# A four-stream counting sort and a reordered tail in a graph-network kernel

## The reference

```
L0:  x += segment_sum(h[src] * e, dst) @ W.T + b
L1:  seg_sum, seg_max, cnt of edge_attr (32 wide) by src;
     x += relu([seg_sum, seg_max, seg_sum/max(cnt,1), u] @ W1 + b1) @ W2 + b2
L2:  hw[r] = h @ weight_r[r];  M = segment_sum(hw[etype, src] / deg[dst], dst)
     x += relu(0.2*h + 0.8*M)
L3:  e = leaky_relu(h@attn_l [src] + h@attn_r [dst]); a = segment softmax of e by dst
     x += elu(segment_sum(h[src] * a, dst))
```

## Time and profile before

| | us |
|---|---|
| median of 3 runs | 22321.71 |
| lowest and highest | 22300.97, 22337.59 |
| the profiled execution, its own time | 22388.18 |
| its span in the trace | 22386.5 |

### The profile page before, as it was taken

One profiled execution on the slowest core, in us unless ns is written; L12 is line 12 of the kernel. 1 busy time (PEld: TensorE's weight loads), 2 busy tenths in 40 slices (PEclk: granted clock), 3 DMA queues, 4 the chain that ended last, 5 costly groups with the idle time before them and its releaser, 6 DMA issues. The chain is left out here.

```text
span 22386.5 us, 124954 instructions
## 1 busy us (share of the span) xinstructions
PE 4204.8 (19%) x27624; PEld 3254.6 (15%) x27624; DVE 7606.3 (34%) x21407; ACT 4300.2 (19%) x11114; POOL 13594.0 (61%) x13464
## 2 busy tenths in 40 slices
PE   1113444444444444211111400000000000000000
PEld 1112333333333333100000300000000000000000
DVE  6663333333333333566655211111111322222222
ACT  0001322222222222222222211111111010110110
POOL 5664444444444444566666377777777677777775
PEclk7555555555555555555555655555555555555555
DMA  2110000000000000133333211111111222222221
GB/s 66 43 43 23 15 17 15 15 15 15 17 15 15 15 15 15 64 97 98 96 99 94 63 48 48 48 44 48 48 44 47 37 45 49 49 46 49 49 45 43
DMA packets 577819, 984.93 MB, mean 44 GB/s; under 512 B 308591, under 2 KB 360528, under 8 KB 541776
## 3 DMA queue, kind: packets, MB, share of 16 engines
q0 software_dynamic: 430432, 388.76, 9.8%
q10 hardware_dynamic: 34560, 436.30, 4.8%
q1 hardware_dynamic: 112368, 155.91, 2.4%
HBM read 458.57 MB, written 521.52 MB: 44 GB/s over the span
## 5 line engine op out<-in xcount | busy, mean ns | idle before, releaser
L725 POOL DMA_INDIRECT by_src<-sort_row,sort_place_i x3240 | 3147.1, 971 | 4108.6 <-DVE sort_place_i L764 3136.7
L363 POOL DMA_INDIRECT rel_G<-rel_table,rel_idx x3240 | 3475.0, 1073 | 1310.8 <-issue 1033.0
L363 POOL DMA_INDIRECT att_G<-att_table,att_idx x3240 | 3403.6, 1050 | 1110.7 <-issue 1110.7
L363 POOL DMA_INDIRECT lead_rows<-h_table,wsum_idx x3120 | 2965.6, 951 | 1718.6 <-issue 935.7
L751 DVE TENSOR_TENSOR sort_before<-pS,below_b 128x128 bf16<-128x128 f32 x3242 | 945.0, 291 | 4505.2 <-remote 3423.5
L862 PE MATMUL pG<-sort_counts,sort_lowTf 128*128 128x98 f32 x6484 | 2133.9, 429 | 0.0
L825 ACT COPY sort_lowT<-pT 128x128 bf16<-128x128 bf16 x3240 | 863.9, 267 | 4478.9 <-remote 1794.7
L862 PEld LDWEIGHTS pG<-sort_counts,sort_lowTf 128*128 128x128 f32 x6484 | 1618.1, 306 | 0.0
L652 PE MATMUL wsum_C<-wsum_high,wsum_low 128*128 128x98 fp8e4 x6480 | 743.8, 264 | 4002.1 <-issue 3231.6
L880 PE MATMUL pT<-ident_b,sort_low 128*128 128x128 bf16 x3240 | 900.5, 278 | 2608.8 <-issue 1507.6
L516 DVE SCALAR_TENSOR_TENSOR rel_Gf<-rel_Sf,rel_keep_first,rel_Gf 128x64 f32<-128x64 f32 x54 | 18.1, 335 | 4001.0 <-ACT rel_Gf L606 2233.3
(11 more groups left out here) (388 smaller groups left out, 12039.5 us busy)
## 6 DMA issues: line engine op xcount, KB each, us to landing
scan_att<-att_S ACTq DMA_DIRECT2D x54, 1980.0 KB
scan_wsum<-wsum_S ACTq DMA_DIRECT2D x54, 1920.0 KB
scan_pool<-pool_S ACTq DMA_DIRECT2D x72, 1440.0 KB
scan_rel<-rel_S ACTq DMA_DIRECT2D x54, 1920.0 KB
pool_row<-by_src SPq DMA_DIRECT2D x36, 1485.0 KB
sort_feat<-in_attr SPq DMA_DIRECT2D x54, 960.0 KB
by_src<-sort_row,sort_place_i POOLq DMA_INDIRECT x3240
rel_G<-rel_table,rel_idx POOLq DMA_INDIRECT x3240
```

The costliest lines, as they stand in the source:

```text
L363: pool.indirect_dma_start(out=G[s][:, j, :], out_offset=None, in_=table, in_offset=bass.IndirectOffsetOnAxis(ap=idx[s][:, j:j + 1], axis=0 ...
L725: pool.indirect_dma_start(out=by_src, out_offset=bass.IndirectOffsetOnAxis(ap=place_i[s][:, j:j + 1], axis=0), in_=row[s][:, j, :], in_off ...
```

## The change

**The sort** is written anew. A step handles four columns (`WAYS = 4`) in 15 steps per chunk. The four have a running table each, side by side in one PSUM bank (`pC`, 128 x 392): column 4g+w uses table w. Table w starts at `first_src` plus the whole counts of tables 0 to w-1 (`streams`), which the counting in wsum now keeps apart. Per chunk, VectorE makes all one-hots at once, `low` 128 x 7680, `high` 128 x 5880, and the transposed one, `lowT`, not by TensorE but by comparing `lows` (the low parts of all 128 partitions' edges, read from DRAM on every partition, one byte each) with the partition's number. The number of partitions above with the same node comes from `keys`: on partition p the src of the 128 partitions before p (16 bits each, -1 above the first), compared with p's own src and summed (`rank_in_tile`). So TensorE's transpose and self-multiplication, ScalarE's two copies and VectorE's mask are gone. The operand with the parts (`parts`, `own_near`) now lies in PSUM. `hand_on` adds the rank and stands at the end of its own chunk. `low` and `high` have one buffer. The row buffers lie in H. SyncE loads `keys` (1.97 MB) and `lows` (0.98 MB) for each chunk when the rank of the chunk before is done.

```diff
+                earlier_keys = bass.AP(tensor=key_rows.tensor, offset=0, ap=[[L, P], [2 * P * L, NCH], [1, P * L]])
+                every_low = bass.AP(tensor=low_rows.tensor, offset=0, ap=[[0, P], [P * L, NCH], [1, P * L]])
...
+                            sp.wait_ge(ranked, k + 1)
+                            sp.dma_start(keys[:].unsqueeze(1), earlier_keys[:, bass.ds(k, 1), :]).then_inc(keys_loaded, 16)
+                            sp.dma_start(lows[:].unsqueeze(1), every_low[:, bass.ds(k, 1), :]).then_inc(keys_loaded, 16)
+                            sp.wait_ge(rows_ready, k + 1)
+                            sp.dma_start(feat[s][:], attr.rearrange("(p j) f -> p j f", p=P)[:, bass.ds(k * L, L), :]).then_inc(loaded[s], 16)
...
-                        pool.wait_ge(place_ready, k + 2)
+                        pool.wait_ge(place_ready, k + 1)
...
+                    def one_hots(k):
+                        dve.wait_ge(ranked, k + 1)
+                        v.tensor_scalar(parts_i[:, 0, :], src_all[:, bass.ds(k * L, L)], 127, None, ALU.bitwise_and)
+                        v.tensor_scalar(parts_i[:, 1, :], src_all[:, bass.ds(k * L, L)], 7, None, ALU.logical_shift_right)
+                        v.tensor_copy(parts[:, 2, :], src_all[:, bass.ds(k * L, L)]).then_inc(split, 1)
+                        dve.wait_ge(split, k + 1)
+                        v.tensor_copy(parts[:, 0:2, :], parts_i[:]).then_inc(parted, 1)
+                        dve.wait_ge(parted, k + 1)
+                        dve.wait_ge(updated, STEPS * k + 1)
+                        part = lambda m, w: parts[:, m, :].unsqueeze(2).to_broadcast([P, L, w])
+                        iota = lambda w: iota_b[:, 0:w].unsqueeze(1).to_broadcast([P, L, w])
+                        v.tensor_tensor(low[:], iota(P), part(0, P), ALU.is_equal)
+                        v.tensor_tensor(high[:], iota(HT), part(1, HT), ALU.is_equal)
+                        dve.wait_ge(keys_loaded, 32 * k + 32)
+                        v.tensor_tensor(lowT[:], lows[:].rearrange("p (x j) -> p j x", j=L),
+                                        own_near.unsqueeze(2).to_broadcast([P, L, P]), ALU.is_equal).then_inc(ones_ready, 1)
+                    def rank_in_tile(k):
+                        by_row = keys[:].rearrange("p (x j) -> p x j", j=L)
+                        v.tensor_tensor(by_row, by_row, parts[:, 2, :].unsqueeze(1).to_broadcast([P, P, L]), ALU.is_equal).then_inc(matched, 1)
+                        dve.wait_ge(matched, k + 1)
+                        v.tensor_reduce(rank[:], keys[:].rearrange("p (x j) -> p j x", j=L), AX, ALU.add).then_inc(ranked, 1)
+                    def weigh(t, n):
+                        dve.wait_ge(summed, t + 3)
+                        dve.wait_ge(placed, t + 1)
+                        g = n % STEPS
+                        v.tensor_tensor(prod[n % 2][:], pG[n % 3][:, 0:W].rearrange("p (w h) -> p w h", w=WAYS),
+                                        high[:, WAYS * g:WAYS * (g + 1), :], ALU.mult).then_inc(picked, 1)
+                    def pick(t, n, s):
+                        dve.wait_ge(picked, t + 4)
+                        g = n % STEPS
+                        v.tensor_reduce(place[s][:, WAYS * g:WAYS * (g + 1)], prod[n % 2][:], AX, ALU.add).then_inc(placed, 1)
+                    def hand_on(k, s):
+                        dve.wait_ge(placed, STEPS * k + (STEPS + 2))
+                        dve.wait_ge(ranked, k + 2)
                         dve.wait_ge(rows_used, k + 2)
-                        v.tensor_copy(place_i[s][:], place[s][:]).then_inc(place_ready, 1)
-                    for tile in (*low, *high, *lowT, *lowTf, *before, *place):
-                        v.memset(tile[:], 0.0)
-                    for b in range(2):
-                        v.tensor_copy(counts[b][:], first_src[:])
-                    v.tensor_copy(ident_b[:], ident[:]).then_inc(cleared, 1)
-                    dve.wait_ge(cleared, 1)
-                    for n in range(AHEAD):
-                        dve.sem_inc(before_ready, 1)
+                        v.tensor_tensor(place_i[s][:], place[s][:], rank[:], ALU.add).then_inc(place_ready, 1)
...
+                    def snapshot(t, n):
+                        act.wait_ge(updated, t + 1)
+                        act.wait_ge(summed, t + 1)
+                        a.copy(cnt[n % 2][:], pC[:, 0:W]).then_inc(snapped, 1)
...
+                    def update(t, g):
+                        pe.wait_ge(snapped, t + 1)
+                        for w in range(WAYS):
+                            last = mm(pC[:, w * HT:(w + 1) * HT], low[:, WAYS * g + w, :], high[:, WAYS * g + w, :],
+                                      start=False, stop=False, skip_group_check=True)
+                        last.then_inc(updated, 1)
+                    def look_up(t, g, n):
+                        pe.wait_ge(picked, t + 1)
+                        for w in range(WAYS):
+                            last = mm(pG[n % 3][:, w * HT:(w + 1) * HT], lowT[:, WAYS * g + w, :], cnt[n % 2][:, w * HT:(w + 1) * HT],
+                                      start=True, stop=True, skip_group_check=True)
+                        last.then_inc(summed, 1)
...
+                            pe.wait_ge(ones_ready, k + 1)
+                            for g in range(STEPS):
+                                t, n = k * STEPS + g, s * STEPS + g
+                                update(t, g)
+                                look_up(t, g, n)
```

**wsum** counts `src` in four streams, prepares `key_rows` and `low_rows` in DRAM, lets GpSimd's gather begin one chunk of counting earlier in the pooled stage, and runs `pool_side` before `count_side` at the stage's end:

```diff
+                        sp.wait_ge(rows_made, 1)
+                        sp.dma_start(key_rows[:, 0:P, :].rearrange("k p j -> p k j"),
+                                     none16[:].unsqueeze(1).to_broadcast([P, NCH, L])).then_inc(rows_stored, 16)
+                        sp.dma_start(key_rows[:, P:2 * P, :].rearrange("k p j -> p k j"), by_chunk(key16)).then_inc(rows_stored, 16)
+                        sp.dma_start(low_rows.rearrange("k p j -> p k j"), by_chunk(low8)).then_inc(rows_stored, 16)
+                        sp.wait_ge(rows_stored, 48)
...
-                            pool.wait_ge(oh_used, 2 * HG * i + (s * HG + 1))
+                            pool.wait_ge(oh_used, 2 * HG * i + (s * HG + 1 - (HG if pooled else 0)))
...
+                        v.tensor_copy(key16, src_all[:, 0:J])
+                        v.tensor_scalar(low_i, src_all[:, 0:J], 127, None, ALU.bitwise_and).then_inc(keys_made, 1)
+                        dve.wait_ge(keys_made, 1)
+                        v.tensor_copy(low8, low_i).then_inc(rows_made, 1)
...
-                    side(NC // 2 - 1, 0)
-                    side(NC // 2 - 1, 1)
+                    for s in range(2):
+                        if pooled:
+                            pool_side(NC // 2 - 1, s)
+                        if counts:
+                            count_side(NC // 2 - 1, s)
...
+                            v.tensor_reduce(count[:], C[:, 0:SW * HT].rearrange("p (w h) -> p h w", w=SW), AX, ALU.add).then_inc(count_ready, 1)
+                            v.tensor_copy(streams[:], C[:, 0:SW * HT].rearrange("p (w h) -> p w h", w=SW))
...
+                                    w = (g * HL + j) % SW
+                                    last = mm(C[:, w * HT:(w + 1) * HT], low[g % NB][:, j, :], high[g % NB][:, j, :],
```

**`first_layers`** moves the carry of wsum to the middle of the groups, gives the load of x its own semaphore, and adds the bias to X behind group 0:

```diff
-                wsum, pooled = Carry("wsum", scan_wsum, D, c, pR), Carry("pool", scan_pool, D, c, pR)
+                wsum, pooled = Carry("wsum", scan_wsum, D, c, pW), Carry("pool", scan_pool, D, c, pR)
+                s_x = semaphore("fl_x", c)
...
+                                     x.rearrange("(h p) d -> p h d", p=P)[:, n * TP:(n + 1) * TP, :]).then_inc(s_x, 16)
...
-                    wsum.vector(dve, st)
+                    dve.wait_ge(s_iota, 1)
+                    for g in range(2):
+                        pooled.select(g, sel, iota_g).then_inc(s_sel, 1)
...
-                    st.done(v.tensor_tensor(X[:], X[:], bias0[:].unsqueeze(1).to_broadcast([P, HT, D]), ALU.add))
...
+                        if g == 0:
+                            dve.wait_ge(s_x, 16 * NPC)
+                            st.done(v.tensor_tensor(X[:], X[:], bias0[:].unsqueeze(1).to_broadcast([P, HT, D]), ALU.add))
                         if g >= 1:
                             add_out(g - 1)
+                        if g == MIDWAY:
+                            wsum.vector(dve, st)
...
-                    wsum.tensor(pe)
...
+                        if g == MIDWAY:
+                            wsum.tensor(pe)
```

219 lines of the change are left out of this document (89 added, 130 removed).

## The result

The changed kernel took 20,197.4 us (median of 4 runs, 20,194.6 to 20,200.6) against 22,311.3 us for the kernel before on the same chip: a ratio of 0.9054, 95% interval 0.9038 to 0.9069. That is faster, by 2114 us where 1467 were forecast, and inside the stated range. The gain belongs to this chip: on another one the kernel before itself took 17,331 us, and there next to nothing was left to gain (last group of experiments).

The account below looks back on a forecast made before the run. GpSimd's scatters wait for places because TensorE gets one record per 1.4 us beside them. Period 85.1 + 21 + 2 = 108 against 134.2 us gives -1383; with -30, -30, -30, +5: 20,920, by medians 20,855 us; range 19,750 to 21,550.

Parts of the forecast that it names:

- The head: Sort, chunk start: VectorE makes one-hots for 29 us with TensorE workless, then the rank for 21.5 us, until 50.5.
- Rival B: Sort: byte and short steps are dear on VectorE; slower past 39.7 us each, 23,650 us at 53 each; chance 0.03.
- 100 records are 4.2 steps: Sort, during the scatter: TensorE's full stock of instructions covers 4.2 steps, done by about 53 us.
- From there 24 x 1.4 = 33.6 us per step: Sort, after the stock: TensorE gets one record per 1.4 us until 85.1 us, one step more, 5.1 done.
- lag 8.5: Sort, after the scatter: TensorE's slow rate outlives the scatter's end by some 8.5 us, until 85.1 us.
- 9.9 steps remain: Sort, after the slow regime: remaining steps take 23.8 us all cold, 18.6 if half warm; 21 us taken.
- rival A: Sort: TensorE is not held in the new loop; period 81 us, kernel 19,440 us; chance 0.12.
- D: Sort: no instruction stock left at 29 us; 1.7 steps in the scatter, period 119, kernel 21,440 us; within main case's 0.84.
- The extras of wsum: Counting in wsum: three more VectorE operations and small-packet writes before stage 1 cost +5 us, bounds 0 and 60.
- Pooled stage: Pooled stage: laxer wait only moves GpSimd's pauses, TensorE's rate still binds; -30 us, bounds -380 and +340.
- Tail and `first_layers`: Pooled stage's end and `first_layers`: reordered side work, moved bias addition and carry save 30 us together, bounds 0 and -60.
- C: Sort: VectorE's large operations hold GpSimd; slower from 28 us on, 23,300 us for all 49; chance 0.01.

Follow-up runs that it names:

- last group of experiments: Changed kernel on a second chip, four edits: places handed on early (after 10 or 13 steps), 40 extra memsets, rank behind step 3; 17,304.0, 17,311.4, 17,310.8, 17,306.1 us.
- the five kernels of the table: Changed kernel (20,197.4 us) and it with look-ups doubled (20,871), look-ups in bf16 (19,747), no rank (20,227), keys and lows loaded in full only once (20,252).
- a close variant of it: Changed kernel plus 40 one-column VectorE memsets per chunk behind the rank, on the second chip: 17,310.8 us.

## Why the prediction was right, and where it was off

**What bounds the kernel.** Right on the first chip: GpSimd waits for places because TensorE's part gets through slowly beside indirect transfers. With more records a step fewer look-ups came ahead of the scatter's end (5.0 for 7.1), with fewer records more (11.3), and the period moved by +12.4 and -8.4 us, the first in good part by TensorE's longer work behind the scatter. 22.7 us less of VectorE and 2.9 MB less of loads moved it by under 1 us. What I did not see is that this belongs to the chip, or to what else differed between the two groups of runs. One trace could not show it. I also laid the old period wholly to the number of records. No run keeps the old one-column step with fewer records, or the new step with the old number, so how the 39.0 us divide between fewer records and fewer hand-overs between engines is not shown.

**The head.** Forecast 29 and 21.5 us, measured 27.5 (8.15 + 6.27 + 13.10) and 22.7 (8.13 + 14.55) and some 1 us of small operations. The rows of L399 and L488 carried over. Rival B would have needed 39.7 us where 13.1 was measured.

**TensorE beside the scatter.** "100 records are 4.2 steps" and "From there 24 x 1.4 = 33.6 us per step" allowed too little: 5.1 steps by 85.1 us, where 7.1 look-ups were through, in the mean, by 76.3. In the chunk shown the two slow steps look alike, ScalarE's copies being 22.6 and 23.1 us apart, but they are not. The first is mostly the wait for VectorE's rank (the look-up ahead of it starts at 3905.49, with the first weigh), and only 4.9 us of it are a late release; the second is late by 22.1 us. Inside these bursts the pace of 1.4 us per record is not seen. The run with doubled look-ups comes near it, with 1.3.

**The period, term by term.** Forecast: scatters 76.6, lag 8.5, steps left 21, end 2, together 108.1. Measured, means of 53 chunks: 76.3, 4.5, 11.5, 2.9, together 95.2. The lag of 8.5 us was carried over from the earlier trace rows. It is the usual one in the old loop, 8.4 to 8.7 us in seven of ten chunks counted; in the new one the first look-up starts 0.1 to 6.2 us after the scatter's end.

**"9.9 steps remain", "I take 21".** This is the term that was off by most, 9.5 of the 12.9 us. At the 2.1 us a step that I took, 4.2 of them are steps: 7.9 remained. The other 5.3 are the price: 1.45 us a look-up. I priced them near the cold bound of 2.4 us each. In the chunk shown the cold ones stand 2.1 us apart (3936.35, 3938.44), the warm ones 1.1, and TensorE had its upper clock from the third on. I had a warm figure, 1.3 a step, from the earlier trace rows, and used it for half at most.

**Sum.** 53 x 12.9 = 684 us are nearly all of the 686 by which the sort beat its forecast of 1383. The direction and the mechanism held. The forecast's middle was 725 us off on the span, a third of the gain, and the range was wide enough because its lower end was built from "no lag, all warm". Small slips in the working: rival A comes by its own terms to 19,424 and the lower end to 20,060, and D prices its steps at 2.4 us where the main case has 2.1.

**The small terms.** First chunk: -30 forecast, -39.6 measured (first cast to first scatter 99.1 for 138.7). The extras of wsum: +5 forecast, -8.2 measured (the first cast comes at 1857.9 for 1866.1). Pooled stage: -30, measured 44 by undoing. Tail and `first_layers`: -30, measured 36 and 0. Together these are 85 forecast and, from the table, 117; the last two by undoing come to 80 where the table has 69, so they overlap or vary by some 11.

**Rivals.** A did not happen on the first chip. On the second the period is A's, just above the scatters, but it seems to hold for both kernels at once, so it does not bring A's 19,440 but removes the gain. Under A the prediction asked whether TensorE gets its instructions too slowly, and the profile's pages bear on that. These are their lines on the queues that load instructions (queue, packets, MB, share), the kernel before first:

```profile
q14 instruction: 435, 3.56, 0.1%
q8 instruction: 24, 0.39, 0.0%
...
q8 instruction: 21, 0.34, 0.0%
q14 instruction: 35, 0.29, 0.0%
```

Of these packets 401 fall between the first and the last scatter of the kernel before, and 5 in the changed one, which has the stall all the same; the runs on the second chip, without it, have 4 or 5. The rule in the Trainium skill ("Runtime: NRT & Kernel Launch", section "Instruction fetch mechanics"), that fetching is mostly hidden, agrees with this: the stall is not the loading of instructions by these queues. What hands the instructions or the signals on so late, no run shows; nor whether the loading, some 7 packets a chunk, cost the old sort time that the new one saves. C is settled by the run with the operand in SBUF. D did not occur: in the chunk above three look-ups and four updates went through at once.

**Open.** Why completions arrive late beside indirect transfers on one chip. What exactly is counted: by the scatter's end TensorE had put through 156 to 200 records in the five kernels of the table, and those whose results VectorE had used were 111 to 157, so neither a fixed number nor a fixed rate fits. Why the changed kernel's chunks fall into two kinds. Whether an early hand-on helps where the stall exists.

## What to carry to other kernels

Count how many instructions have to get through on TensorE while GpSimd issues indirect transfers, and put them where it is idle; then ask for a second chip before believing the size of the gain. Give every large two-input VectorE operation that runs beside GpSimd one operand in PSUM: one line was worth 1550 us here. To price a stretch, decide by the trace which clock its last instructions had; here a burst of nine steps had the upper one back in its third. And count over all chunks before one is taken for typical: here a third of them ran another way than the one shown.

## What the runs showed of the hardware that was not expected

- The same program took 22,288 to 22,335 us on one chip and 17,331 on another, with the 0.97 us of a scatter unchanged. For the changed kernel and a close variant of it, where the scatters' stretch took 5118.5 and 4123.8 us, the difference lies in waits between engines and in shorter gathers (L2's have a mean of 1068 and 947 ns).
- Beside indirect transfers on the first chip, TensorE's bursts ran without gaps (eight f32 passes in 1.99 us), but their consumers on VectorE and ScalarE were released up to 22 us late, the last of them 0.3 and 4.6 us after the last transfer's end.
- Each of four VectorE operations with two SBUF inputs held one GpSimd transfer until 0.8 us after its own end: 8.11, 5.88, 12.68 and 7.80 us beside 8.16, 6.28, 13.10 and 8.15. With one of the inputs in PSUM the longest of the 3240 transfers took 1.01 us, and beside L818, with a single input, one took 0.97.
- A byte read at steps of 60 bytes cost 1.71 ns per element on VectorE, and a 16-bit number at 120 bytes, summed, 1.89 ns, hardly more than an f32 at 256 bytes (1.72).
